# A fused transformer kernel on one NeuronCore: first attention with three packed projections, four moved row sets a block and late division

## The chip, the cores and the metric

The kernel runs on one core of a Trainium2 chip. The metric is the device time of one execution in microseconds; the kernel before takes 709.20 us (median of three runs, 709.16 to 710.09).

## What is computed

x is 16 sequences of 256 tokens with 128 features, all float32. Four layers follow each other, each added to x: an attention (a), a gated feed-forward, a second causal attention with 16 heads, and the same feed-forward again. Only the first attention and the preparation of the feed-forward's weights are touched. The reference of the first, cut:

```
x = x + attn_a(layernorm(x), Wq, bq, Wk, bk, Wv, bv, Wo, bo, freq)
q, k, v = (x @ W + b) split in 2 heads of 64
q, k: features 0..31 of a head stay (content), features 32..63 are rotated (spatial)
      [x1, x2] -> [x1*cos - x2*sin, x1*sin + x2*cos], x1 and x2 of 16 features
score = q k^T / sqrt(64);  attn = softmax(score);  out = (attn v) @ Wo + bo
```

The feed-forward's weights are split into a high and a low part (`whi`, `wlo`) while the first attention runs, and it is counted whether any low part differs from zero.

## The kernel before

x lies in SBUF. The work goes in 8 blocks of two sequences (512 tokens, `TOK`); a block b has two sets of scores, s = 0 and 1, one a sequence. Each engine has its own program, written out by hand (`pe_body`, `act_body`, `dve_body`, `pool_body`), and meets the others at semaphores. A body of block b finishes b, prepares b+1 and begins b+2: `run_inner` runs the bodies of blocks 1 to 6 (1 to 4 in a loop), `..._program` holds what comes before, with the body of block 0, and the last block's part. The queues are in order, so the order of the calls in a body is the order of the work.

In a body of TensorE (`pe_body`, matmuls L220, transposes L449 and L212): scores (b, 1), the k projection of b+1, the transposes of the probabilities (b, 0), k's swapped projection, values (b, 0), v of b+1, the output projection of b-1, scores (b+1, 0), the transposes of xn of b+2, the probabilities (b, 1), two q projections of b+2, values (b, 1). q and k each have two projections: one plain and one with the weight columns of the rotation's halves swapped (`WQR`, `WKR`). VectorE multiplies the first by a cosine row (`straight`, L637) and the second by a sine row (`turned`, L642), GpSimd adds the two (L766). The content features have cosine 1 and sine 0, so they go through all of it.

The softmax: VectorE takes the maxima (L652) and negates and scales them (L657), ScalarE the exponentials with their sums (L553), VectorE the reciprocals (L661), then VectorE normalises head 0 (L666) and ScalarE head 1 (L568), TensorE transposes and ScalarE copies (`act_probT`, L561). There is one set of score banks, so the next scores wait for the exponentials. x of the block gets the output in one add (`dve_update`, L673), and `bo` on GpSimd (L774). Layer norm of b+2: statistics on VectorE (L171, L174), rstd on GpSimd (L207), the shift on VectorE (L189), application on ScalarE (L198, 4 instructions). The weights come in 8 pieces of 704 columns through two stage buffers: ScalarE rounds (L846), GpSimd subtracts (L851), VectorE counts (L857) and writes into the stage buffer while it does, after which SP loads the next piece.

## Time and profile before

| | before |
|---|---|
| median of 3 runs | 709.20 us |
| profiled execution, its time | 709.26 us |
| its span, first to last instruction | 707.5 us |
| mean granted TensorE clock | 0.986 |
| busy, share of the span: TensorE, VectorE, ScalarE, GpSimd | 92%, 70%, 64%, 60% |
| first attention | from the start to about 130 us |

The span is the time of the profiled execution less what lies around it. Busy times of TensorE are modelled at their ends: the distance between two starts says more than a drawn length.

### The profile page before, as it was taken

Reading aid. Unit: us, or ns where it says so; the run is one execution under the profiler, and the core shown is the slowest. Engines: PE = TensorE matmul, PEld = TensorE weight load, DVE = VectorE, ACT = ScalarE, POOL = GpSimd, SP = SyncE. Lnnn points to the kernel's source line nnn. Section 1 sums busy time; section 2 is a strip of 40 time slices with the busy share of each in tenths; the row PEclk is TensorE's granted clock in tenths of the full one; section 3 lists DMA queues with packets and bytes.
Section 4 is the critical chain, followed back from the end, with each engine's and each line's share of the span. In section 5 each row is a group of like instructions: output and inputs, shape, how many; then the busy total and the mean of one; then the engine's idle time right before and its main releaser. Section 6 shows DMA issues by size and latency. Waiting matters only on the chain.

```text
span 707.5 us, 14026 instructions
## 1 busy us (share of the span) xinstructions
PE 652.9 (92%) x4713; PEld 455.8 (64%) x4716; DVE 498.2 (70%) x958; ACT 450.7 (64%) x801; POOL 425.5 (60%) x443
## 2 busy tenths in 40 slices
PE   3789998799999999997999999998989999999997
PEld 1455555477777877675555555555546777787785
DVE  6879998676556778466778888877678565776521
ACT  3678886546665566545676677776765565666664
POOL 4545543368778777533346645654666877778673
PEclk9999999899999999998999999999999999999999
DMA  6101230000000000560467666664221000000001
GB/s 197 41 22 42 54 42 1 1 0 2 1 0 0 0 1 1 188 229 3 138 198 241 198 224 216 224 220 151 84 87 35 0 16 15 15 0 16 16 15 31
DMA packets 33028, 52.47 MB, mean 74 GB/s; under 512 B 4560, under 2 KB 9680, under 8 KB 32976
## 3 DMA queue, kind: packets, MB, share of 16 engines
q1 hardware_dynamic: 32784, 51.53, 23.3%
q8 instruction: 30, 0.49, 0.3%
q10 hardware_dynamic: 192, 0.26, 0.1%
q14 instruction: 22, 0.18, 0.1%
HBM read 27.15 MB, written 24.38 MB: 73 GB/s over the span
## 4 chain that ended last, share of the span: by engine, by line
PE 64%; DVE 16%; ACT 8%; issue 7%; DMA 2%; POOL 2%; DVEq 1%; ACTq 0%; POOLq 0%
PE banks L220 61%; ACT b_prob L1525 4%; DVE xn L182 3%; DVE a_mx L652 2%; ACT a_prob L553 2%; PE banks L212 1%; DVE f_gate L1088 1%; DVE f_h_hi L1091 1%; DVE a_prob L666 1%; DVE f_hidden L1094 1%; PE banks L977 1%; DVE a_straight L637 1%; DVE w_stage L857 1%; ACT f_g_hi L1044 1%; DVE stats L171 1%
## 5 line engine op out<-in xcount | busy, mean ns | idle before, releaser
L1158 POOL TENSOR_TENSOR f_g_lo<-f_gelu,f_g_hi 128x512 fp32r<-128x512 f32 x127 | 162.9, 1292 | 54.1 <-ACT f_g_hi L1044 53.6
L1043 ACT ACTIVATE f_gelu<-banks,cols 128x512 f32<-128x512 f32 x128 | 88.3, 690 | 132.5 <-PE banks L220 110.6
L1624 DVE TENSOR_REDUCE b_segment_max<-banks 128x6 f32<-128x768 f32 x128 | 120.0, 950 | 27.6 <-PE banks L220 27.0
L1741 POOL TENSOR_SCALAR_AFFINE_SELECT b_prob<-b_prob 128x512 f32<-128x512 f32 x128 | 81.7, 639 | 89.2 <-ACT b_prob L1525 88.5
L220 PE MATMUL banks<-f_g_hi,whi 128*128 128x512 f32 x320 | 130.2, 407 | 1.9 <-POOL f_g_lo L1158 1.4
L220 PE MATMUL banks<-f_g_lo,whi 128*128 128x512 f32 x320 | 126.7, 396 | 0.0
L1525 ACT ACTIVATE b_prob<-banks 128x768 f32<-128x768 f32 x128 | 102.4, 807 | 37.5 <-PE banks L220 37.2
L1151 POOL TENSOR_TENSOR f_h_lo<-f_hidden,f_h_hi 128x512 fp32r<-128x512 f32 x60 | 77.6, 1294 | 61.2 <-DVE f_hidden L1094 58.5
L220 PE MATMUL banks<-f_h_hi,whi 128*128 128x512 f32 x256 | 105.2, 411 | 6.2 <-POOL f_h_lo L1151 3.4
L220 PE MATMUL banks<-f_h_lo,whi 128*128 128x512 f32 x256 | 102.0, 398 | 0.0
L1044 ACT ACTIVATE f_g_hi<-banks,cols 128x512 fp32r<-128x512 f32 x128 | 87.4, 683 | 0.0
L1088 DVE SCALAR_TENSOR_TENSOR f_gate<-f_tanh,banks 128x512 f32<-128x512 f32 x64 | 43.3, 677 | 51.5 <-ACT f_tanh L1035 51.5
L220 PE MATMUL banks<-f_xn_split,whi 128*128 128x512 f32 x256 | 71.8, 403 | 1.7 <-DVE f_hidden L1094 1.3
L220 PEld LDWEIGHTS banks<-f_g_hi,whi 128*128 128x128 f32 x320 | 60.3, 188 | 17.2 <-POOL f_g_lo L1158 3.1
L182 DVE TENSOR_SCALAR xn<-X,mv,rstd 128x128 f32<-128x128 f32 (+1 forms) x104 | 70.5, 743 | 0.6 <-POOL rstd L207 0.4
L220 PEld LDWEIGHTS banks<-f_g_lo,whi 128*128 128x128 f32 x320 | 60.3, 189 | 13.2 <-issue 0.2
L220 PEld LDWEIGHTS banks<-f_h_hi,f_h_lo 32*128 32x128 f32 x512 | 37.3, 185 | 43.3 <-ACT b_prob L1525 35.4
L220 PE MATMUL banks<-f_h_hi,f_h_lo 32*128 32x256 f32 (+1 forms) x512 | 55.5, 301 | 8.9 <-ACT b_prob L1525 6.1
L220 PEld LDWEIGHTS banks<-f_h_hi,whi 128*128 128x128 f32 x256 | 48.7, 190 | 23.2 <-POOL f_h_lo L1151 4.5
L220 PEld LDWEIGHTS banks<-f_xn_split,whi 128*128 128x128 f32 x256 | 48.2, 191 | 15.2 <-DVE f_hidden L1094 2.0
L220 PE MATMUL banks<-b_prob,b_values 128*16 128x256 f32 (+1 forms) x1024 | 55.8, 331 | 0.6 <-POOL b_prob L1741 0.6
L220 PEld LDWEIGHTS banks<-f_h_lo,whi 128*128 128x128 f32 x256 | 48.6, 190 | 11.2 <-issue 0.5
(125 smaller groups left out, 1096.4 us busy)
## 6 DMA issues: line engine op xcount, KB each, us to landing
f_h_hi<-b_q_dram SPq DMA_DIRECT2D x16, 512.0 KB, 4.1
f_h_lo<-b_k_dram SPq DMA_DIRECT2D x16, 512.0 KB, 5.2
b_o_dram<-b_o SPq DMA_DIRECT2D x8, 1024.0 KB, 4.4
b_q_dram<-b_q_hi SPq DMA_DIRECT2D x16, 256.0 KB, 3.3
b_k_dram<-b_k_hi SPq DMA_DIRECT2D x16, 256.0 KB, 3.0
w_stage<-in_wF SPq DMA_DIRECT2D x8, 352.0 KB, 3.2
b_q_dram<-b_q_lo SPq DMA_DIRECT2D x8, 256.0 KB, 3.4
b_k_dram<-b_k_lo SPq DMA_DIRECT2D x8, 256.0 KB, 3.1
```

Source lines behind the costliest of these rows:

```text
L182: nc.vector.tensor_scalar(xn[:, s, :], X[:, bass.ds(TILES * t + s, 1), :], mv[:, s, 0:1], rstd[:, s:s + 1], ALU.subtract, ALU.mult).then_i ...
L220: return nc.tensor.matmul(out, lhsT, rhs, start=start, stop=stop)
L553: last = nc.scalar.activation(prob[s][:, h, qt, :], score[:, h, qt * T:(qt + 1) * T], ACT.Exp, bias=nm[s][:, h, qt:qt + 1], scale=SCALE_A, ...
L652: nc.vector.reduce_max(mx[s][:, :, :], score[:, :, :].rearrange("p h (q k) -> p h q k", q=2), AX.X).then_inc(s_mx, 1)
L1043: nc.scalar.activation(gf[c % 2][:, :], z_bank[c % 2], ACT.Gelu, scale=scale).then_inc(s_gf, 1)
L1044: nc.scalar.activation(hi[:, c, :], z_bank[c % 2], ACT.Gelu, scale=scale).then_inc(s_ghi[c % 2], 1)
L1088: nc.vector.scalar_tensor_tensor(out=uu[slot][:, :], in0=th[slot][:, :], scalar=1.0, in1=a[:, :], op0=ALU.add, op1=ALU.mult).then_inc(s_u, 1)
L1151: nc.gpsimd.tensor_tensor(hlo[n.odd][:, c, :], hf[c % 2][:, :], hhi[n.odd][:, c, :].bitcast(F32), ALU.subtract).then_inc(s_hlo[c % 2], 1)
L1158: nc.gpsimd.tensor_tensor(lo[:, c, :], gf[c % 2][:, :], hi[:, c, :].bitcast(F32), ALU.subtract).then_inc(s_glo[c % 2], 1)
L1525: nc.scalar.activation(prob[n % 2][:, p, :, :, :], second_banks(b, p)[:, :, 0:3 * P].rearrange("p b (c q) -> p c b q", c=3), ACT.Exp, scal ...
L1624: nc.vector.reduce_max(seg[:, g, s, 2 * p:2 * p + 2, :], first_pass[:, 2 * p:2 * p + 2, 0:3 * P].rearrange("p b (c k) -> p b c k", c=3), A ...
L1741: nc.gpsimd.affine_select(out=pr, in_=pr, compare_op=ALU.is_ge, fill=0.0, base=0, pattern=[[0, 4], [1, P]], channel_multiplier=-1).then_in ...
```

## The change

Layout: the weights and biases of q and k are packed by kind of feature. One 128-column projection gives the content features of q and k of both heads, one the spatial ones, one the spatial ones with their halves swapped. The first is biased and scaled by ScalarE into `content`; the other two go through VectorE and GpSimd into `spatial`. The factor 1/8 of the scores is multiplied into q's rows by these steps. SP then moves the rows of q and k to the even and odd partitions of `qT` and `kT` in four SBUF-to-SBUF transfers a block (`sp_moves`, 64 partitions by 512 floats, 128 KB each), on whose landing the block's first scores wait.

Softmax: the probabilities are never normalised. The maximum comes out negated. The output projection is done head by head (contraction over 64 rows) into two banks, and x is updated with each, times the head's reciprocal sum as a scalar (8 instructions of 128 columns). The two updates hold the banks that the next content and spatial projections write (`s_half`, `s_done`).

Beside that: the norm's shift is made on GpSimd, from a negated mean; the weight count writes to an unused buffer, so a stage buffer is free once GpSimd has read it; pieces 0 and 1 are rounded ahead of block 0, but subtracted on GpSimd in the middle of block 0 and counted on VectorE at its end. Transfers of the pieces stand in SP's queue behind the moves of a block, and the constant rows of the second attention behind all moves.

```diff
             def sp_program(sp):
...
+                blocks = [Block(i // 2, i % 2) for i in range(BLOCKS)]
+                for n in blocks:
+                    sp_moves(sp, n)
+                    if n.t >= 1:
+                        for piece in blocks[2:4] if n.t == 1 else blocks[n.t + 2:n.t + 3]:
+                            ffn["sp_piece"](sp, piece, False)
...
+            def sp_moves(sp, n):
+
+                t = n.t
+                wait(sp, s_sc, SEQS * (t - 1))
+                sp.wait_ge(s_co, t + 1)
+                for i, to in enumerate((qT, kT)):
+                    sp.dma_start(to[n.odd][0:P:2, :], content[HALF_P * i:HALF_P * (i + 1), :]).then_inc(s_mc, 16)
+                sp.wait_ge(s_ro, t + 1)
+                for i, to in enumerate((qT, kT)):
+                    sp.dma_start(to[n.odd][1:P:2, :], spatial[HALF_P * i:HALF_P * (i + 1), :]).then_inc(s_ms, 16)
...
             def pe_scores(pe, b, s):
                 if s == 0:
-                    pe.wait_ge(s_ro, 2 * (b.t + 1))
+                    pe.wait_ge(s_mc, 16 * MOVES * (b.t + 1))
+                    pe.wait_ge(s_ms, 16 * MOVES * (b.t + 1))
...
             def pe_probT(pe, b, s, h):
-                pe.wait_ge(s_no[h], SEQS * b.t + s + 1)
+                pe.wait_ge(s_ex, UNITS * b.t + HA * s + h + 1)
...
                 pe.wait_ge(s_oc, b.t + 1)
-                token_major(bank, oT, wA[:, WO, :]).then_inc(s_y, 1)
...
+                for s in range(TILES):
+                    for h, bank in enumerate((bank0, bank1)):
+                        at = slice(DA * h, DA * (h + 1))
+                        last = mm(bank[:, s * P:(s + 1) * P], oT[at, s * P:(s + 1) * P], wA[at, WO, :])
+                last.then_inc(s_y, 1)
...
                 if two:
-                    pe_proj(pe, n2, "qr")
-                    pe_proj(pe, n2, "q")
+                    pe_swapped(pe, n2)
+                    if before:
+                        pe.wait_ge(s_half, b.t)
+                    pe_content(pe, n2)
+                    if before:
+                        pe.wait_ge(s_done, b.t)
+                    pe_spatial(pe, n2)
...
                 if two and not is_block(b, 0):
                     ffn["beside"]["act"](act, n2)
-                act_normalise(act, b, 0)
-                if before:
-                    act_out(act, b.after(-1))
-                for h in (1, 0):
+                for h in range(HA):
                     act_probT(act, b, 0, h)
...
+            def dve_update(dve, b, h, bank):
+
                 dve.wait_ge(s_y, b.t + 1)
-                dve.wait_ge(s_bo, b.t + 1)
-                nc.vector.tensor_tensor(xblk(b.t), tiles_of(bank), xblk(b.t), ALU.add).then_inc(s_done, 1)
+                dve.wait_ge(s_in_, b.t + 1)
+                dve.wait_ge(s_half if h else s_bo, b.t + 1)
+                for s in range(TILES):
+                    x = X[:, bass.ds(TILES * b.t + s, 1), :]
+                    last = nc.vector.scalar_tensor_tensor(
+                        out=x, in0=tiles_of(bank)[:, s:s + 1, :], scalar=inv[b.odd][:, s // 2, h, s % 2:s % 2 + 1],
+                        in1=x, op0=ALU.mult, op1=ALU.add)
+                last.then_inc(s_done if h else s_half, 1)
...
                 if is_block(b, 0):
-                    ffn["beside"]["dve"](dve, n2)
+                    ffn["beside"]["dve"](dve, b)
+                    ffn["beside"]["dve"](dve, n1)
...
+                if is_block(b, 0):
+                    ffn["beside"]["pool"](pool, b)
+                    ffn["beside"]["pool"](pool, b.after(1))
+                elif two:
                     ffn["beside"]["pool"](pool, b.after(2))
                 if two:
-                    pool_rope(pool, b.after(2), 0)
+                    pool_rope(pool, b.after(2))
```

How the instructions now stand, at the two places that matter most. TensorE, one whole body inside the bodies of blocks 1 to 6, from the scores (b, 1) on (`a_kT,a_qT` are scores, `xnT,wA` projections of q and k, `wA,xnT` that of v, `wA,a_oT` the output projection). Before:

```order
L220 MATMUL banks<-a_kT,a_qT 128x256 x4
L220 MATMUL banks<-xnT,wA 128x512
L449 MATMUL banks<-ident,a_prob 128x128 x8
L220 MATMUL banks<-xnT,wA 128x512
L220 MATMUL banks<-a_probT,a_v 64x256 x4
L220 MATMUL banks<-wA,xnT 128x128 x4
L220 MATMUL banks<-wA,a_oT 128x128 x4
L220 MATMUL banks<-a_kT,a_qT 128x256 x4
L212 MATMUL banks<-ident,xn 128x128 x4
L449 MATMUL banks<-ident,a_prob 128x128 x8
L220 MATMUL banks<-xnT,wA 128x512 x2
L220 MATMUL banks<-a_probT,a_v 64x256 x4
```

And with the change:

```order
L223 MATMUL banks<-a_kT,a_qT 128x256 x4
L472 MATMUL banks<-ident,a_prob 128x128 x8
L223 MATMUL banks<-wA,xnT 128x128 x4
L223 MATMUL banks<-a_probT,a_v 64x256 x4
L223 MATMUL banks<-wA,a_oT 128x128 x8
L223 MATMUL banks<-a_kT,a_qT 128x256 x4
L215 MATMUL banks<-ident,xn 128x128 x4
L472 MATMUL banks<-ident,a_prob 128x128 x8
L223 MATMUL banks<-xnT,wA 128x512 x3
L223 MATMUL banks<-a_probT,a_v 64x256 x4
```

The two projections that stood around the first transposes are gone, one is added to the pair at the end, and the output projection has eight matmuls in place of four.

VectorE, the body of block 5 (behind the loop). Before, its first half:

```order
L661 RECIPROCAL a_inv<-a_total 128x4
L171 BN_STATS stats<-X 128x6 x4
L174 BN_AGGR mv<-stats 128x2 x4
L666 TENSOR_SCALAR a_prob<-a_prob,a_inv 128x256 x2
L652 TENSOR_REDUCE a_mx<-banks 128x4
L189 SCALAR_TENSOR_TENSOR shift<-mv,rstd 128x4
L657 TENSOR_SCALAR a_nm<-a_mx 128x4
L637 SCALAR_TENSOR_TENSOR a_straight<-banks,cols,cosines 128x512
```

With the change, the whole body:

```order
L174 BN_STATS stats<-X 128x6 x4
L177 BN_AGGR mv<-stats 128x2 x4
L687 TENSOR_REDUCE a_nm<-banks 128x4
L681 TENSOR_TENSOR a_v<-banks,rows 128x512
L692 RECIPROCAL a_inv<-a_total 128x8
L872 TENSOR_SCALAR f_h_hi,f_lo_in_piece<-wlo 128x704
L701 SCALAR_TENSOR_TENSOR X<-banks,a_inv,X 128x128 x4
L687 TENSOR_REDUCE a_nm<-banks 128x4
L701 SCALAR_TENSOR_TENSOR X<-banks,a_inv,X 128x128 x4
L667 SCALAR_TENSOR_TENSOR a_turned<-banks,cols,sines 128x512
L675 SCALAR_TENSOR_TENSOR a_straight<-banks,cols,cosines 128x512
```

The maximum now follows the statistics directly, and the two updates of x enclose the second maximum.

## Rows read from the trace of the kernel before

**Rows 1.** Windows view, bodies 0, 1, 2 to 5 and 6: busy (instructions) by engine.
```profile
core 0: us, PE busy (x) PEld busy (x) DVE busy (x) ACT busy (x) POOL busy (x), PEclk, DMA share, GB/s
24.87:38.00 13.13, 11.68 (x68) 6.70 (x68) 10.41 (x28) 9.94 (x30) 4.56 (x6) 1.00 0.17 55
38.00:54.73 16.73, 13.87 (x79) 8.58 (x77) 12.73 (x29) 11.57 (x33) 8.21 (x7) 0.90 0.10 24
54.73:107.29 52.56, 50.17 (x304) 30.61 (x305) 48.85 (x109) 43.60 (x124) 26.64 (x24) 1.00 0.27 46
107.29:121.06 13.77, 10.98 (x75) 7.17 (x75) 11.56 (x31) 8.93 (x26) 6.25 (x6) 1.00 0.00 0
```
**Rows 2.** Timeline, TensorE, regular body: start us, length us, instruction, idle before.
```profile
83.00 1.04 PE L449 MATMUL banks<-ident,a_prob 128*128 128x128 f32 x8
83.88 1.02 PE L220 MATMUL banks<-xnT,wA 128*128 128x512 f32 x2
...
90.11 1.09 PE L449 MATMUL banks<-ident,a_prob 128*128 128x128 f32 x8 [0.25 <-DVE a_prob L666]
91.03 1.88 PE L220 MATMUL banks<-xnT,wA 128*128 128x512 f32 x4
92.85 1.08 PE L220 MATMUL banks<-a_probT,a_v 128*64 128x256 f32 x8
```
**Rows 3.** Timeline, TensorE, behind the gap of body 1, where nothing holds it.
```profile
46.19 1.08 PE L220 MATMUL banks<-a_probT,a_v 128*64 128x256 f32 x8
...
48.20 1.06 PE L220 MATMUL banks<-wA,a_oT 128*128 128x128 f32 x8
49.19 1.13 PE L220 MATMUL banks<-a_kT,a_qT 64*128 64x256 f32 x8
50.25 0.66 PE L212 MATMUL banks<-ident,xn 128*128 128x128 f32 x4
50.74 1.08 PE L449 MATMUL banks<-ident,a_prob 128*128 128x128 f32 x8
```
**Rows 4.** Timeline, VectorE, regular body.
```profile
82.37 0.58 DVE L666 TENSOR_SCALAR a_prob<-a_prob,a_inv 128x256 f32<-128x256 f32 x2
...
84.00 1.19 DVE L189 SCALAR_TENSOR_TENSOR shift<-mv,rstd 128x4 f32<-128x4 f32 x1
...
88.02 2.03 DVE L666 TENSOR_SCALAR a_prob<-a_prob,a_inv 128x256 f32<-128x256 f32 x2
...
93.45 0.74 DVE L637 SCALAR_TENSOR_TENSOR a_straight<-banks,cols,cosines 128x512 f32<-128x512 f32 x1
```
**Rows 5.** Timeline, GpSimd, regular body: the add of q's two products.
```profile
94.27 1.27 POOL L766 TENSOR_TENSOR a_qT<-a_straight,a_turned 128x512 f32<-128x512 f32 x1 [4.63 <-DVE a_straight L637]
```
**Rows 6.** Timelines, VectorE and TensorE, handover to the feed-forward.
```profile
124.83 0.66 DVE L673 TENSOR_TENSOR X<-banks,X 128x512 f32<-128x512 f32 x1
...
126.61 1.11 DVE L182 TENSOR_SCALAR xn<-X,mv,rstd 128x128 f32<-128x128 f32 x4
...
125.54 2.14 PE L220 MATMUL banks<-f_xn_split,whi 128*128 128x512 f32 x8 [0.33 <-DVE X L673]
```
**Rows 7.** Timeline, ScalarE, regular body: copies, first exponential, applications.
```profile
83.64 1.08 ACT L561 ACTIVATE a_probT<-banks 128x512 f32<-128x512 f32 x2 [0.76 <-PE banks L449]
85.39 0.47 ACT L553 ACTIVATE a_prob<-banks,a_nm 128x256 f32<-128x256 f32 x1 [0.66 <-DVE a_nm L657]
...
87.20 1.65 ACT L198 ACTIVATE xn<-X,shift,rstd 128x128 f32 x4
```
**Rows 8.** DMA issues of the page: count, KB each, median us to landing.
```profile
f_h_lo<-b_k_dram SPq DMA_DIRECT2D x16, 512.0 KB, 5.2
...
b_k_dram<-b_k_hi SPq DMA_DIRECT2D x16, 256.0 KB, 3.0
...
cols<-in_cols SPq DMA_DIRECT2D x1, 13.5 KB, 1.8
```
**Rows 9.** Timelines, VectorE and TensorE, the gap in body 1.
```profile
40.85 0.89 DVE L857 TENSOR_SCALAR_CACHE_REDUCE w_stage<-wlo 128x704 f32<-128x704 f32 x1 [3.01 <-POOL wlo L851]
...
42.92 1.97 PE L449 MATMUL banks<-ident,a_prob 128*128 128x128 f32 x8 [2.73 <-ACT a_prob L568]
```

More of the change, by code:

```diff
@@ L579, in act_body @@
                 nxt = link["next"]
+                if before:
+                    act_out(act, b.after(-1))
                 if two and not is_block(b, 0):
                     ffn["beside"]["act"](act, n2)
-                act_normalise(act, b, 0)
-                if before:
-                    act_out(act, b.after(-1))
-                for h in (1, 0):
+                for h in range(HA):
                     act_probT(act, b, 0, h)
@@ L598, in act_body @@
                     act_exp(act, n1, 0)
+                if two:
+                    act_content(act, n2)
                 if is_block(b, 0):
@@ L663, in dve_normalise @@
[L663 to L673 removed]
+                wait(dve, s_ex, UNITS * (b.t - 1) + HA * (s + 1))
@@ L677, in dve_body @@
                 nxt = link["next"]
-                if not two:
-                    ffn["dve_total"](dve)
-                dve_inverse(dve, b, 0)
                 if two:
@@ L696, in dve_body @@
                     nxt["norm"].dve_apply(dve, FIRST_BLOCK, True)
-                if one:
-                    dve_v(dve, n1)
-                dve_normalise(dve, b, 1)
                 if before:
-                    dve_update(dve, b.after(-1))
+                    dve_inverse(dve, b.after(-1))
+                if two and not is_block(b, 0):
+                    ffn["beside"]["dve"](dve, n1)
+                if before:
+                    dve_update(dve, b.after(-1), 0, content_bank)
                 if one:
                     dve_max(dve, n1, 0)
-                    dve_negate(dve, n1, 0)
-                if two and not is_block(b, 0):
-                    ffn["beside"]["dve"](dve, n2)
+                if before:
+                    dve_update(dve, b.after(-1), 1, spatial_bank)
                 if two:
-                    dve_rope(dve, n2, "qr")
-                    dve_rope(dve, n2, "q")
+                    dve_swapped(dve, n2)
+                    dve_spatial(dve, n2)
                 else:
@@ L774, in pool_body @@
                 nc.gpsimd.tensor_tensor(xblk(b.t), xblk(b.t), row4("bo"), ALU.add).then_inc(s_bo, 1)
-                if one:
-                    pool_rope(pool, b.after(1), 1)
-                if two and not is_block(b, 0):
+                if is_block(b, 0):
+                    ffn["beside"]["pool"](pool, b)
+                    ffn["beside"]["pool"](pool, b.after(1))
+                elif two:
                     ffn["beside"]["pool"](pool, b.after(2))
                 if two:
-                    pool_rope(pool, b.after(2), 0)
+                    pool_rope(pool, b.after(2))
                 if is_block(b, 0):
```

308 lines of the change are left out of this document (144 added, 164 removed).

## The prediction, made before the changed kernel was run

> **What bounds the kernel now.** I cut the first attention into bodies, from one block's second scores to the next block's, at the starts of the score matmuls, and read the windows view of them [rows 1]. Body 0 takes 13.13 us, body 1 takes 16.73 us, the four bodies 2 to 5 take 52.56 us (13.14 us each), body 6 takes 13.77 us. Nothing behind 130 us is touched by the change except one update of x, so the answer lies in these seven bodies, the lead-in and the handover to the feed-forward.
>
> Then the timeline of a regular body. TensorE starts one group after the other with little idle time shown [rows 2], and VectorE is busy 48.85 of 52.56 us [rows 1]. Both are close to full, so I ask what each does when nothing holds it. The distance from start to start gives a group's price. Unheld, the groups cost: a projection 0.91 us (1.82 for two), the transposes of two probabilities 0.88 and 0.92 [rows 2], a value product with the v projection 2.01 (about 1.00 each), the output projection 0.99, scores 1.06, the transposes of xn 0.49 [rows 3]. A body now holds two scores (2.12), four projections (3.64), the probabilities' transposes (1.80), two value products (2.00), v (1.01), the output (0.99) and xn's transposes (0.49): 12.05 us. So 1.09 of 13.14 us are waits, and VectorE causes them: it normalises two tiles in 2.03 us where the same work takes 0.58 in the other half of the body, and its tiny shift takes 1.19 us [rows 4].
>
> **The change, part by part.** *Projections.* Three wide ones instead of four: TensorE loses 0.91 us a body, VectorE two of its four rotation steps (0.74 us each [rows 4]), GpSimd one add of 1.27 us [rows 5].
>
> *Normalisation.* Gone are VectorE's 2.03 + 0.58 us, its negations and shift (1.19 us), and ScalarE's two pairs. In their place x is updated by eight 128-wide steps from PSUM where one 512-wide step took 0.66 us. Four 128-wide steps of another kind took 1.11 us [rows 6], so I take 2.2 us for the eight; the bounds are 1.3 us (eight quarters of 0.66) and 5.3 us (eight of 0.66). VectorE's body becomes 48.85/4 = 12.2, less 2.61 for the normalisation, 1.19 for the shift and 1.48 for the rotations, plus 2.2 - 0.7 for the update: about 8.4 us. It stops being the bound at any value under the upper bound.
>
> *Output projection by heads.* Eight matmuls with 64 rows of contraction instead of four with 128; in the trace each fp32 matmul is two weight loads and two passes, so 16 of each instead of 8. No row shows this shape. The scores are the nearest: 64-row matmuls of the two heads, 8 passes of 256 columns in 1.06 us [rows 3], less than 8 such passes would take one behind the other (a 512-column projection has two passes in 0.91 us, so a 256-column pass takes 0.23 us and eight take 1.8 us). So the two heads run side by side, and the output should take what it took, 0.99 us. Bounds: 0.9 us and 2.1 us (16 at the scores' 0.13 us per pass). The Trainium skill, TensorE: Matmul & The Clock Gate, section LDWEIGHTS, speaks against this part: a load takes as long as it has columns, however few its rows (128 columns: an estimate of 0.107 us by its formula), so 16 loads one after the other would take 1.7 us, and the sum would be 3 us smaller. The scores' rows decide for me.
>
> *The body as it will be.* TensorE's own work is 12.05 - 0.91 = 11.14 us. The other closed path is that of xn: its transposes 0.49, probabilities' transposes 0.92, three projections 2.73, value product 1.00, scores 1.06, then 0.64 until ScalarE copies the next probabilities (83.00 to 83.64), two copies 1.08, exponentials 1.81 (85.39 to 87.20), four applications 1.65 [rows 7], hand-over 0.05 (an estimate): 11.43 us. ScalarE's copies stand ahead of the exponentials in its queue, and xn behind them, which is why this path is longer than TensorE's own. **I take 11.43 us a body.** With an update at its upper bound VectorE would need 11.5 us, about the same.
>
> *Four transfers a block.* The rows of q and k go from SBUF to SBUF, and the next scores wait for them; SP's queue holds nothing but these and one weight piece behind them. From the spatial projection to the scores that need it TensorE has 0.91 + 1.00 + 1.06 + 0.88 + 1.01 + 1.00 + 0.99 = 6.85 us of other work, 7.14 us with the 0.29 us by which the body exceeds its own work. Of that go about 1.1 us until VectorE has the product (a projection is drawn 1.02 us long [rows 2]), 0.82 to GpSimd's start (93.45 to 94.27), 1.27 for its add [rows 4, 5], and an estimate of 0.45 us for the first of the two issues. A landing of up to 3.5 us is therefore hidden. This kind of transfer of 128 KB is not in the trace. Bounds: 1.8 us (13.5 KB) and 5.2 us (512 KB); 256 KB take 3.0 us [rows 8]. I take 2.3 us, hidden with about 1 us to spare.
>
> *Weight pieces in block 0.* Before, GpSimd's late piece holds VectorE for 3.01 us, that holds ScalarE's normalisation, and TensorE stands 2.73 us; the granted clock is 0.90 over this body, and the transposes behind the gap are drawn 1.97 us long, not 1.04 to 1.09 [rows 1, 2, 9]. Now VectorE checks the two old pieces at the end of block 0, which puts 2 x 0.89 us [rows 9] ahead of the next statistics and maximum. An estimate of 0.5 us of it is slack (the statistics end that much before the exponentials' queue is free), so what is late next are the exponentials of body 1, by 1.3 us.
>
> *Sum, with bodies as in [rows 1].* Body 0: 13.13 to 11.43, -1.7. Body 1: 16.73 to 12.75, -4.0. Bodies 2 to 5: 4 x (13.14 - 11.43) = -6.8. Body 6: the transposes for the feed-forward now wait until both halves of an earlier x update are done, and VectorE comes to the second only behind a piece check, statistics, two maxima and the feed-forward's four applications, some 9.5 us after the start. TensorE has 3 us of nothing there, ScalarE's last exponentials come late, and the body ends at 13.8 us as before; 0. The clock fell after the 2.73 us gap in body 1 before, so I add 0.5 us here. Lead-in: the first scores now wait for transfers, +0.2. Handover: the gate products start at 125.54, released by the x update [rows 6]. That update is 2.2 instead of 0.66 us, with little else changed ahead of it: +1.3. The last update, in the feed-forward, has idle VectorE time behind it; 0. Together -1.7 - 4.0 - 6.8 + 0.5 + 0.2 + 1.3 = **-10.5 us**. The profiled execution took 709.26 us (span 707.5), 0.06 us from the median 709.20, so the forecast is 709.3 - 10.5 = 698.8 us.
>
> **Rivals.** *(a) The split output projection pays for each load*: up to its bound of 2.1 us in place of 0.99. TensorE's own 11.14 becomes 12.25 us, 0.8 above the 11.43 path, in six bodies: 4.9 us lost, 703.7. Against it stands the scores' price. It is the mechanism that the Trainium skill's section on LDWEIGHTS would give. *(b) The moves are too slow by a little*: landing at 4 to 4.5 us costs 0.5 to 1.0 us in seven places: 702.3 to 705.8. *(c) Slower than before: the moves set the pace.* From a landing of 3.5 us on, each further microsecond lengthens all seven waits for q and k; at 5.0 us the 10.5 us are used up, and at the 5.2 us of the 512 KB row, with 0.1 us more for the second transfer, the time is 698.8 + 7 x 1.8 = 711.4. For it: two transfers are queued together, beside a 352 KB piece. Against: the size is a quarter of that row's. *(d) The change does not do what it says in block 0*: the gap only moves, since three pieces on GpSimd and two on VectorE still stand before the statistics. Then body 1 stays at about 16 us and the total is 702. *(e) More than forecast*: the xn path is overlapped better, the clock stays up at the handover, and a body is TensorE's bare 11.14 us: 6 x 0.29 + 0.5 + 1.3 = 3.5, so 695.3.
>
> **How the numbers follow.** Forecast 0.52; (a) 0.12; (b) 0.11; (c) 0.05; (d) 0.10; (e) 0.10. A measurement of this kernel can tell a change of about 0.2%, 1.4 us, from none. Faster by more takes the forecast, (a), (d), (e) and nearly all of (b), 0.92; (b)'s slow end gives 0.03 for no difference; (c) gives 0.05. For 8 in 10 I go from 694.5 (e with a little more) to 704.5, which takes in (a), (d) and most of (b).
>
> **What would show it.** In the changed profile: score matmuls (second of a block) 11.3 to 11.7 us apart in bodies 2 to 5; the group of 16 output passes (rows name it wA, a_oT) near 1.0 us from start to start; the moves landing in 2 to 3 us and no wait of TensorE on them; VectorE near 8.6 us a body; no idle of 2.7 us in body 1 and a granted clock of 1.00 there; the handover's update released later than now. I am wrong if TensorE waits for the moved rows in each body, if the output group takes 1.7 us or more, or if bodies 2 to 5 stay above 12.5 us.

## The result, and the profile after

The changed kernel takes 705.79 us (median of 16 runs, 703.44 to 709.21), the kernel before 709.18 us in the same series (16 runs, 707.23 to 710.37). The ratio is 0.9953, with an interval of 0.9941 to 0.9966: faster, by 3.4 us, where 10.5 us were forecast. The time lies above the range.

The profiled execution took 704.96 us (span 703.1, mean granted clock 0.982, before 0.986). TensorE is busy 92% of it as before, VectorE 68% (70%), ScalarE 63% (64%), GpSimd 59% (60%).

First the windows view of the changed kernel, cut at the same instructions as [rows 1]: bodies 0, 1, 2 to 5, 6, and below them the handover, from the second scores of block 7 to the first gate products.
```profile
core 0: us, PE busy (x) PEld busy (x) DVE busy (x) ACT busy (x) POOL busy (x), PEclk, DMA share, GB/s
26.87:38.37 11.50, 10.26 (x68) 6.57 (x67) 5.96 (x15) 10.33 (x29) 7.38 (x9) 1.00 0.43 109
38.37:51.21 12.84, 11.47 (x84) 7.48 (x83) 10.29 (x30) 10.07 (x29) 7.29 (x8) 1.00 0.29 71
51.21:96.73 45.52, 44.65 (x331) 29.57 (x329) 34.95 (x97) 39.04 (x112) 22.71 (x29) 1.00 0.29 71
96.73:112.51 15.78, 10.53 (x81) 7.40 (x79) 10.56 (x29) 7.82 (x23) 4.89 (x5) 0.84 0.53 87
112.51:120.72 8.21, 6.73 (x41) 4.89 (x41) 4.78 (x19) 3.02 (x10) 1.22 (x2) 0.68 0.47 51
```
Set beside [rows 1], and with the handover of before (121.06 to 125.54, 4.48 us):

| stretch | before | forecast | after | off by |
|---|---|---|---|---|
| lead-in, to block 0's second scores | 24.87 | 25.1 | 26.87 | +1.8 |
| body 0 | 13.13 | 11.43 | 11.50 | +0.1 |
| body 1 | 16.73 | 12.75 | 12.84 | +0.1 |
| bodies 2 to 5 | 52.56 | 45.7 | 45.52 | -0.2 |
| body 6 | 13.77 | 14.3 (0.5 for the clock) | 15.78 | +1.5 |
| handover | 4.48 | 5.8 | 8.21 | +2.4 |
| gate products start at | 125.54 | 115.0 | 120.72 | +5.7 |

The bodies came out as forecast: the terms of bodies 0, 1 and 2 to 5 are right within 0.2 us. What is missing up to the gate products lies in the three stretches at the ends. Two of them show a granted clock (PEclk) below 1.00 here, and so does the lead-in, below.

The timeline of TensorE in a regular body of the changed kernel (start, length, instruction, idle time before it in brackets):
```profile
54.19 1.08 PE L223 MATMUL banks<-a_probT,a_v 128*64 128x256 f32 x8
55.20 1.16 PE L223 MATMUL banks<-wA,a_oT 64*128 64x128 f32 x16
56.20 1.03 PE L223 MATMUL banks<-a_kT,a_qT 64*128 64x256 f32 x8
57.45 0.66 PE L215 MATMUL banks<-ident,xn 128*128 128x128 f32 x4 [0.21 <-ACT xn L199]
57.94 1.04 PE L472 MATMUL banks<-ident,a_prob 128*128 128x128 f32 x8
58.81 2.82 PE L223 MATMUL banks<-xnT,wA 128*128 128x512 f32 x6
```
Sixteen passes of 64 rows take 1.00 us from start to start (55.20 to 56.20), what eight passes of 128 rows took in [rows 3] (0.99). The only wait in this body is one of 0.21 us. From the page's DMA part of bodies 2 to 5, count, size and median us to landing of the content moves (the two spatial ones: 2.2 and 2.3):
```profile
a_qT<-a_content SPq DMA_DIRECT2D x4, 128.0 KB, 2.2
a_kT<-a_content SPq DMA_DIRECT2D x4, 128.0 KB, 2.4
```
Next the lead-in, TensorE's timeline of the changed kernel:
```profile
18.44 0.66 PE L215 MATMUL banks<-ident,xn 128*128 128x128 f32 x4 [1.41 <-DVE a_v L681]
21.38 1.28 PE L223 MATMUL banks<-a_kT,a_qT 64*128 64x256 f32 x8 [2.29 <-DMA a_kT<-a_spatial]
22.60 4.34 PE L223 MATMUL banks<-xnT,wA 128*128 128x512 f32 x6
26.87 1.14 PE L223 MATMUL banks<-a_kT,a_qT 64*128 64x256 f32 x8
```
and the first and the last of SP's four issues for block 0 that these scores wait for:
```profile
17.05 0.55 SPq L379 DMA_DIRECT2D a_qT<-a_content  x1
...
18.91 0.60 SPq L382 DMA_DIRECT2D a_kT<-a_spatial  x1
```
TensorE stands 2.29 us for the last of them. Then six passes of a projection take 4.34 us where the same six take 2.82 in the regular body: the granted clock went to its lower level at 22.2 us, for 3.4 us.

Last, the end of body 6 and the handover, TensorE:
```profile
106.81 0.66 PE L215 MATMUL banks<-ident,xn 128*128 128x128 f32 x4 [3.64 <-DVE X L701]
107.30 1.65 PE L472 MATMUL banks<-ident,a_prob 128*128 128x128 f32 x8
...
109.73 1.98 PE L223 MATMUL banks<-a_probT,a_v 128*64 128x256 f32 x8 [0.66 <-ACT a_probT L602]
112.51 2.08 PE L223 MATMUL banks<-a_kT,a_qT 64*128 64x256 f32 x8 [0.80 <-issue]
114.52 1.97 PE L472 MATMUL banks<-ident,a_prob 128*128 128x128 f32 x8
116.42 1.81 PE L223 MATMUL banks<-wA,a_oT 64*128 64x128 f32 x16
118.16 1.08 PE L223 MATMUL banks<-a_probT,a_v 128*64 128x256 f32 x8
120.72 2.14 PE L223 MATMUL banks<-f_xn_split,whi 128*128 128x512 f32 x8 [1.48 <-DVE X L701]
```
and a windows view of TensorE there, cut at the granted clock:
```profile
103.00:107.60 4.60, 0.96 (x9) 1.00 0.46 49
107.60:117.80 10.20, 8.74 (x45) 0.50 0.46 50
```
The wait of 3.64 us that the prediction had seen ("TensorE has 3 us of nothing there") is followed by 10.2 us at 1.2 GHz instead of 2.4. Transposes take 1.65 and 1.97 us (1.04 in the regular body), a value product 1.98 (1.08), scores 2.08 (1.03), output 1.81. I had put 0.5 us on this. VectorE's update that the gates wait for is 2.38 us long (118.28, eight steps; 2.2 priced); four such steps take 1.12 us.

### The profile page after: what moved, and what is told of

Its sections match the earlier page's. It is cut to its first block, busy times and chain, and to the rows that moved or that the text cites. A ratio compares the mean times of both kernels' runs of the same rounds, so it can differ in the third digit from the quotient of the medians.

```text
span 703.1 us, 14140 instructions
## 1 busy us (share of the span) xinstructions
PE 647.1 (92%) x4761; PEld 455.7 (65%) x4764; DVE 477.4 (68%) x937; ACT 442.2 (63%) x777; POOL 417.1 (59%) x448
## 4 chain that ended last, share of the span: by engine, by line
PE 65%; DVE 7%; ACT 7%; issue 4%; POOL 1%; DMA 1%; ACTq 0%; DVEq 0%; POOLq 0%
PE banks L223 62%; ACT b_prob L1540 4%; DVE xn L185 2%; DVE f_gate L1103 1%; DVE f_h_hi L1106 1%; PE banks L215 1%; PE banks L992 1%; ACT f_g_hi L1059 1%; DVE f_hidden L1109 1%; DMA f_h_hi<-b_negative_max 1%; DVE X L701 1%; ACT f_tanh L1050 1%; POOL f_g_lo L1173 1%; DVE b_segment_max L1639 1%; PE banks L472 0%
```

## Experiments

Twelve kernels were run, in four series. Each series had its own runs of the kernel before (medians 708.29, 709.65, 708.64 and 708.98 us), so the kernels are compared by their ratios to it. The last column is the ratio's distance from the changed kernel's 0.9953, times 709.2 us; its uncertainty is 1 to 2 us, since each ratio has an interval of 0.0012 to 0.0025 to either side. Differences of fill_lead, order1 and flag_late from the changed kernel, and of bank_const from bank, are within or at the edge of that. The last two columns are of one profiled execution each. "Last body and handover" runs from block 6's second scores to the gate products in the profile.

| kernel | median us | ratio [interval] | block 0's second scores | last body and handover | against the changed kernel |
|---|---|---|---|---|---|
| changed | 705.79 | 0.9953 [0.9941, 0.9966] | 26.87 | 23.99 | |
| fill_both | 702.27 | 0.9917 [0.9904, 0.9929] | 25.87 | 22.52 | -2.6 |
| fill_lead | 705.17 | 0.9936 [0.9922, 0.9949] | 25.44 | 24.91 | -1.2 |
| fill_six | 703.91 | 0.9921 [0.9899, 0.9943] | 26.99 | 23.71 | -2.3 |
| order1 | 706.55 | 0.9973 [0.9958, 0.9988] | 26.77 | 23.94 | +1.4 |
| bank | 702.34 | 0.9921 [0.9902, 0.9939] | 27.73 | 20.58 | -2.3 |
| flag_late | 705.48 | 0.9946 [0.9932, 0.9960] | 26.57 | 22.43 | -0.5 |
| bank_flag | 702.20 | 0.9878 [0.9859, 0.9897] | 28.40 | 18.38 | -5.3 |
| bank_flag_fill | 697.26 | 0.9831 [0.9815, 0.9847] | 25.63 | 17.77 | -8.7 |
| two_queues | 697.91 | 0.9843 [0.9824, 0.9862] | 25.88 | 17.77 | -7.8 |
| bank_const | 700.94 | 0.9900 [0.9876, 0.9925] | 26.16 | 17.74 | -3.8 |
| best_const | 697.80 | 0.9837 [0.9823, 0.9851] | 24.80 | 18.33 | -8.2 |
| before_pieces | 712.82 | 1.0070 [1.0056, 1.0084] | 24.82 | (19.13) | |

The kernel before has 24.87 us and 18.25 us in these two columns. bank_flag's five runs lie in two groups (699.5 to 699.9 and 702.2 to 702.5 us), so its figure is the least certain: the ratio of the medians is 0.9895, 4.1 us below the changed kernel.

### Does the clock take the gain? fill_both, fill_lead, fill_six

```diff
+ def pe_fill(n):
+     for _ in range(n):
+         mm(pT_bank[0], ident[:, :], wA[:, 0:4, :].rearrange("p w e -> p (w e)"))
...
+                pe_fill(2)
                 pe_scores(pe, b0, 0)
...
                 else:
+                    pe_fill(3)
                     pe.wait_ge(s_done, b.t)
                     nxt["pe_T"](pe, FIRST_BLOCK)
```


> Extra TensorE work whose results nobody reads: two 512-column matmuls (identity by projection weights) before the first scores, three before the feed-forward's first transposes in body 6; all waits stay as in the changed kernel. Clock theory (the halved clock, not the waits, costs most of what was lost against the forecast): granted clock 1.00 from 16 to 125 us, scores (0,1) at 26.1 instead of 26.87 us, the gate products 2.2 to 3 us earlier than the changed kernel's 120.72, time about 702.8 us, and the runs lie closer together. Wait theory (the moved rows and the x update hold TensorE, whatever its clock): scores (0,1) stays at 26.9, the gates move by under 0.5 us, time 705.5.

> The changed kernel with the two dummy products ahead of the first scores alone (of the experiment fill_both, which had three more in body 6 and came to 702.27 us). Theory (the two clock falls cost separately: about 1 us of the lead-in, 2.5 us of body 6 and the handover): second scores of block 0 at 25.9 us instead of 26.87, the clock fall at 106 to 108 us stays with its 10 us, time 704.6 to 705.0 us. Rival (all of the gain of fill_both was the lead-in, the rest was chance): time 702.3 us. Other rival (all of it was body 6): 705.8 us.

> The changed kernel with the three dummy products ahead of the feed-forward's first transposes in body 6 alone, waits unchanged. fill_lead alone came to 705.17 us, both together to 702.27, the changed kernel to 705.79. Theory (nearly all of the gain of fill_both is that the clock does not fall for 10 us behind the wait of 3.64 us): no fall between 104 and 110 us, body 6 of 14.3 to 15.2 us instead of 15.78, time 703.0 to 703.6 us. Rival (the clock falls anyway somewhat later, behind the flag's load of 1.6 us, unless the lead-in is filled as well): time 704.5 to 705.5 us.

The program of all three keeps every wait for a semaphore; dummy work fills part of the idle time. In fill_both the clock fell neither in the lead-in nor at 104 to 110 us, and the time dropped by 0.36% (2.6 us, with an uncertainty of 1.3). The clock fell at 111.4 instead, for 3.4 us, behind a new wait ahead of block 7's second scores ([1.63 <-issue]). fill_lead brought the second scores of block 0 forward by 1.43 us (0.45 of it because the whole execution started earlier: first projections at 10.79, not 11.24), as the theory had it; in body 6 the clock then fell earlier, at 103.9, and the last body and handover took 0.9 us longer. fill_six took the wait before the transposes from 3.64 to 0.86 us with the clock up, and the fall came at 111.6, for 6.8 us:
```profile
106.90 0.66 PE L215 MATMUL banks<-ident,xn 128*128 128x128 f32 x4 [0.86 <-DVE X L706]
...
109.31 1.08 PE L223 MATMUL banks<-a_probT,a_v 128*64 128x256 f32 x8 [0.76 <-ACT a_probT L607]
112.05 2.08 PE L223 MATMUL banks<-a_kT,a_qT 64*128 64x256 f32 x8 [1.66 <-issue]
```
Body 6 of fill_six, from the second scores of block 6 to those of block 7:
```profile
96.82:112.05 15.23, 11.79 (x86) 7.71 (x85) 10.56 (x29) 7.50 (x23) 4.89 (x5) 0.99 0.53 89
```
With the clock up it still takes 15.23 us (fill_both: 15.21), 0.55 less than the 15.78 of the changed kernel. The transposes come 10.08 us after its start here, in fill_both and in the changed kernel, so the length of the wait does not hang on the clock, and most of what body 6 lost is not the clock's.

The falls of the clock that fill_both removed thus cost about 2.6 us. Its theory had the gate products (118.19, 2.5 us earlier) and the time right, but not a clock of 1.00 up to 125 us. For fill_six the rival (the fall comes anyway, later) had the mechanism right, the theory was nearer with the time. What is new is the wait put down to "issue".

### The order of the lead-in: order1

```diff
                 pe_T(pe, b1)
-                pe_scores(pe, b0, 0)
                 pe_swapped(pe, b1)
                 pe_spatial(pe, b1)
+                pe_scores(pe, b0, 0)
                 pe_content(pe, b1)
```
(ScalarE's content of block 1 and VectorE's two rotation steps moved ahead likewise.)

> Lead-in reordered: block 1's swapped and spatial projections stand before the first scores, its content is scaled before the first exponentials. Both theories: TensorE has work while the moved rows of block 0 are under way. Clock theory: no fall of the clock at 22 us, scores (0,1) at about 26.0 instead of 26.87, and the next wait for moved rows (1.24 us before scores (1,0)) goes too: 1 to 2 us less than the changed kernel, 704.3. Wait theory: the first scores still start at 21.4 or later, since the transfers end then; only the 1.24 us wait goes, 704.8.

No gain (ratio 0.9973), though both theories had forecast one. Block 1's projections fill the wait for the moves, and that of 1.24 us before scores (1,0) went too, but everything behind the first scores is then bare: the second scores, at 26.77, stood 2.69 us for the exponentials, and the clock fell at 27.2 instead. In the profiles, dummy work in the gap brought the second scores to 25.44 (fill_lead) where real work moved into it did not.

### Body 6's wait for the x update: bank

```diff
-                    pe_out(pe, b.after(-1))
+                    if two: pe_out(pe, b.after(-1))
+                    else:
+                        pe.wait_ge(s_vr, BLOCKS)
+                        pe_out(pe, b.after(-1), content_bank, misc)
...
                 else:
-                    pe.wait_ge(s_done, b.t)
                     nxt["pe_T"](pe, FIRST_BLOCK)
...
-                else:
-                    pe.wait_ge(s_vr, BLOCKS)
-                    ffn["pe_total"](pe)
                 pe_pv(pe, b, 1)
+                if not two:
+                    pe.wait_ge(s_done, b.t)
+                    ffn["pe_total"](pe)
```


> In body 6 the second head's output product goes to the bank of v's product instead of the one into which the feed-forward's first transposes go, so these no longer wait for the x update; the count of low parts moves behind the value product. Wait theory: the transposes start at about 103.4 instead of 106.81 us, the last exponentials of score set (7,0) 3.7 us earlier, the clock does not fall (no idle of 3.6 us), the gate products start at about 113.5 instead of 120.72, time 699 us. Clock theory alone, without a part for the wait: the same transposes' start but at most 3 us gained, 703 us. If a different wait takes its place (the exponentials or the application of the norm), under 1 us is gained.

The 3.64 us are gone, and the last body with the handover takes 20.58 us instead of 23.99. Up to the gate products this profile gains 2.5 us of these 3.4, since in this execution the clock was down for 6.8 us in the lead-in; by the ratio the time fell by 2.3 us. Of the theories neither came out whole: the wait is gone, but another took its place. TensorE of bank:
```profile
106.62 1.08 PE L223 MATMUL banks<-a_probT,a_v 128*64 128x256 f32 x8 [0.88 <-ACT a_probT L605]
107.70 0.19 PE L223 MATMUL banks<-f_ones,f_lo_in_row 128*1 128x1 f32 x2
110.90 1.29 PE L223 MATMUL banks<-a_kT,a_qT 64*128 64x256 f32 x8 [3.01 <-issue]
```
A wait of 3.01 us now stands ahead of block 7's second scores, and the clock fell at 111.8 behind it, for 3.4 us. Between the two groups TensorE's queue loads the flag that says whether any low part of a weight is not zero.

### The flag's load: flag_late, bank_flag, bank_const

flag_late and bank_flag move the load in TensorE's program:
```diff
-                ffn["pe_load_flag"](pe)
                 pe_scores(pe, LAST_BLOCK, 1)
                 for h in range(HA):
                     pe_probT(pe, LAST_BLOCK, 0, h)
+                ffn["pe_load_flag"](pe)
```


> The changed kernel with one step of TensorE's queue moved: the load of the flag (whether any low part of a weight is not zero) stands behind the second scores of block 7 and the transposes after them, no longer ahead. Theory (the load holds TensorE's queue: VectorE's cast of the flag ends at 109.26 us, and the scores come at 112.51, of which 0.80 us is idle time put down to issue): the scores come about 0.8 us earlier, the clock fall of 107.6 stays, and the end comes 0.5 to 1 us earlier, 705 us. Rival (the gap is that of the exponentials of block 7, which free the score bank at 111.2, and the load only moves the wait): the scores move by no more than 0.2 us or the output group behind the load waits instead, and the time stays at 705.8 us.

> The kernel of the experiment bank (body 6 hands the second head's output group to another bank, so that the feed-forward's transposes do not wait for the x update) with the flag's load moved behind the second scores of block 7 and their transposes. In bank TensorE was idle for 3.01 us before these scores (107.9 to 110.9), and its clock fell at 111.8 for 3.4 us. Theory (the idle time is the flag's load, and the clock fall follows from it): scores at about 108.6 us (the exponentials of block 7 end at 108.55), no clock fall near 112, gate products at 114.5 to 115.5 instead of 118.20, time about 699 us. Rival (the load takes its 2.8 us wherever it stands in the queue): the gap turns up before the output group of block 6 instead, gates at 117.5 or later, time 701.5 to 702.5 us.

Both did the step that was claimed. In flag_late the scores follow the value product at once (111.62, no wait), 15.21 us after block 6's second scores instead of 15.78, so 0.57 us earlier and not 0.8; the time, 0.5 us less, cannot be told from none. In bank_flag the distance from block 7's first scores to its second fell from 7.97 to 5.71 us, and the last body with the handover from 20.58 to 18.38. The clock fell all the same at 109.3, for 3.4 us, so my "no clock fall" was wrong, and the handover kept 7.36 us.

How long the load holds the queue shows in its own rows: of the kernel before,
```profile
L1931 PEldq TENSOR_LOAD <-f_lo_anywhere x1: 489/489/489, 119.2 to 119.2; - x1
```
of the changed one,
```profile
L1946 PEldq TENSOR_LOAD <-f_lo_anywhere x1: 2230/2230/2230, 109.9 to 109.9; - x1
```
(ns, start in us). One instruction, one number, and 1.74 us longer. What changed beside it is SP's queue. Of the kernel before and of the changed one:
```profile
80.46 0.34 SPq L285 DMA_DIRECT2D wB<-in_wB  x1
...
84.53 4.63 SPq L289 DMA_DIRECT2D b_k_dram<-b_constant_rows  x1
```
```profile
99.09 0.58 SPq L288 DMA_DIRECT2D wB<-in_wB  x1
...
103.07 4.65 SPq L292 DMA_DIRECT2D b_k_dram<-b_constant_rows  x1
```
The second attention's constants are issued behind all that SP does for the first. Before, that was one weight piece at 79.9 us; now it is the moves of block 7 at 98 us. The transfers then run for some 20 us (the DMA share is 0.50 from 100 to 120 us, and was 0.00 from 110 to 125 before), over the flag's load. bank_const holds them back until block 7's second scores are done:
```diff
                             ffn["sp_piece"](sp, piece, False)
+                sp.wait_ge(s_sc, SEQS * BLOCKS)
```


> The kernel of bank with one wait more at the end of SP's program: the five transfers of the second attention's constants (the last two issues take 2.6 and 4.6 us on SP, and the transfers run on for some 20 us) start only when the second scores of block 7 are done. Before the change they stood at 80.5 to 102 us; in the changed kernel SP reaches them only behind the last moves, at 99 us, so that they lie over the flag's load, which took 0.49 us before and 2.20 to 2.30 us in every kernel with the change. Theory (the load is slow because these transfers are under way): load of 0.5 us, idle time ahead of the second scores of block 7 down from 3.01 to about 1.2 us (scores 1.8 us earlier behind the value product), time 0.5 to 1.8 us below bank's 702.3. Rival (the load is slow for another reason, its place in the program or the state of TensorE's queue): load of 2.2 us again, gap 3 us, time 702.3.

```profile
L1950 PEldq TENSOR_LOAD <-f_lo_anywhere x1: 486/486/486, 106.6 to 106.6; - x1
```
The theory stands for the load: 0.49 us again, and the idle time ahead of the scores is 1.20 us instead of 3.01. The time is 1.5 us below bank's by the ratios, which is inside the uncertainty of 2.2. Windows view of body 6 and the handover in bank_const:
```profile
96.01:107.48 11.47, 9.15 (x80) 6.69 (x79) 10.56 (x29) 7.61 (x23) 4.89 (x5) 1.00 0.20 46
107.48:113.75 6.27, 4.27 (x41) 3.03 (x41) 4.78 (x19) 2.91 (x10) 1.22 (x2) 1.00 0.41 75
```
Here the handover runs with a clock of 1.00 and a short load, and still takes 6.27 us, not the 5.8 of the forecast. VectorE sets it, without a gap between the reciprocal and the update:
```profile
111.05 0.17 DVE L696 RECIPROCAL a_inv<-a_total 128x8 f32<-128x8 f32 x1
111.31 2.38 DVE L705 SCALAR_TENSOR_TENSOR X<-banks,a_inv,X 128x128 f32<-128x128 f32 x8
```
The update starts 3.83 us after the second scores (3.77 in the kernel before, 5.77 in the changed one), and the gates start 2.44 us after it (0.71 in the kernel before, 2.44 in the changed one).

The Trainium skill, DMA: Bandwidth & Descriptors, section Latency and other measured facts, gives a load of this kind a floor of about 0.6 us. The rows show less, 0.49 us with the transfer engines quiet and 2.2 to 2.3 us beside those transfers; how they delay it (a shared ring, or the memory) no run here tells.

### Putting the parts together: bank_flag_fill, two_queues, best_const

bank_flag_fill is bank_flag with the two dummy products of the lead-in.

> bank_flag with two dummy products of 128x512 ahead of the first scores, which compute nothing that is used and fill the wait for the moves of block 0. Theory (part of what the lead-in lost is TensorE's clock, which fell at 22.2 us behind the wait of 2.29 us and at 19.6 us for 6.8 us in the profile of bank): no clock fall before 100 us, second scores of block 0 at 25.9 us instead of 26.9 to 27.7, and all later bodies as much earlier; time 1 to 1.8 us below that of bank_flag, about 697.5 us. Rival (the lead-in waits for the moves and for ScalarE, whatever the clock): within 0.4 us of bank_flag.

```profile
95.46:106.48 11.02, 9.14 (x80) 6.68 (x79) 10.52 (x29) 7.17 (x23) 4.89 (x5) 1.00 0.57 104
106.48:113.23 6.75, 4.33 (x41) 3.03 (x41) 4.82 (x20) 3.35 (x11) 1.22 (x2) 1.00 0.46 51
```
The clock is at its upper level up to 124 us, and the kernel takes 697.26 us: 0.9831 [0.9815, 0.9847] of the kernel before, faster than both. It is 3.3 us below bank_flag by the ratios (with an uncertainty of 1.8), where 1 to 1.8 were expected. In the two profiles the gate products come 3.4 us earlier: 2.8 of it is the lead-in (28.40 to 25.63; bank_flag's clock was down there for 6.8 us) and 0.6 the handover (7.36 to 6.75 us), which kept the full clock too. One wait shows where the flag's load went:
```profile
109.59 1.16 PE L223 MATMUL banks<-wA,a_oT 64*128 64x128 f32 x16 [0.95 <-issue]
...
113.23 2.14 PE L223 MATMUL banks<-f_xn_split,whi 128*128 128x512 f32 x8 [1.46 <-DVE X L709]
```
two_queues lets ScalarE issue block 0's two content moves, with one dummy product instead of two:
```diff
                 act_content(act, FIRST_BLOCK)
+                act.wait_ge(s_co, 1)
+                for i, to in enumerate((qT, kT)):
+                    act.dma_start(to[0][0:P:2, :], content[HALF_P * i:HALF_P * (i + 1), :]).then_inc(s_mc, 16)
```


> bank_flag_fill with the two content moves of block 0 issued by ScalarE's queue instead of SP's, and one dummy product of 0.94 us ahead of the first scores instead of two. In the changed kernel the four issues of block 0 follow one another on SP (17.05, 17.64, 18.28 and 18.91 us), and the last lands 2.36 us after its start, at 21.27. Theory (the queue of issues sets the first scores): the spatial moves start at 17.3 and 17.9, the last lands at about 20.2, first scores at 20.2 to 20.4 us (bank_flag_fill: 21.21), second ones about 0.9 us earlier, no clock fall in the lead-in; time 0.6 to 1.0 us below bank_flag_fill, about 696.5. Rival (ScalarE's later work, delayed by its two issues of 0.6 us each, sets the next step): second scores at 25.4 us or later, time within 0.3 us of bank_flag_fill. Other rival (transfers issued at once share the engines and land later): first scores at 21 us.

The other rival came out. The four issues went out in 1.5 us instead of 2.5, two and two at once, but three of them took longer to land (DMA issues of this stretch, the queue in the second column, the last number us to landing):
```profile
a_qT<-a_spatial SPq DMA_DIRECT2D x1, 128.0 KB, 2.3
a_qT<-a_content ACTq DMA_DIRECT2D x1, 128.0 KB, 3.1
a_kT<-a_content ACTq DMA_DIRECT2D x1, 128.0 KB, 3.3
a_kT<-a_spatial SPq DMA_DIRECT2D x1, 128.0 KB, 3.0
```
From the end of ScalarE's content step to the first scores it is 3.99 us (17.46 to 21.45) instead of 4.36, and that step itself came 0.44 us later in this execution. That the four transfers share the engines is the rival's reason; the rows show the longer landings alone. First scores and second scores (25.88) are where bank_flag_fill has them within 0.3 us, and no gain can be told.

best_const adds the held-back constants to bank_flag_fill.

> bank_flag_fill (697.26 us) with the same wait for the second attention's constants. Theory: load of the flag 0.5 us instead of 2.25, the idle time of 0.95 us ahead of block 6's output group gone, gate products 6.75 - 0.95 = 5.8 us behind the second scores of block 7, time about 696.4 us. Rival (the load stays at 2.2 us): 697.3 us. If the constants, now between 107 and 130 us, get in the way of the feed-forward's first blocks (they share no engine with it but the SP queue and the transfer engines), the time is above 697.3.

The load took 0.49 us and the wait of 0.95 us is gone, but the clock fell at 106.0, for 3.4 us, behind waits of 0.88 and 0.74 us that bank_flag_fill has as well without a fall, and the handover took 7.32 us. By bank_const's 6.27 the 5.8 of this theory was out of reach even at the full clock. The time, 697.80 us, cannot be told from 697.26.

### The piece order alone: before_pieces

The kernel before, with VectorE's check of each weight piece one body later (as in the change), and nothing else.

> The kernel before with one part of the change alone: VectorE counts a weight piece one body later, so body 1 does not begin with a wait for GpSimd's piece. If the gap in body 1 is a matter of this order alone: no idle of 2.7 us, granted clock 1.00 at 42 us, body 1 at 13.1 to 13.5 us instead of 16.73, time 705.9 us, equal to the whole gain of the full change. If the gap only moves (another engine waits for the same piece): over 708 us.

It is slower than the kernel before, by 0.7%, over the 708 us of the second theory; whether by its mechanism is open. The gap of [rows 9] is gone, the clock stays up, and body 1 takes 14.40 us instead of 16.73. But bodies 2 to 5 take 56.53 us instead of 52.56:
```profile
37.95:52.35 14.40, 12.80 (x78) 7.55 (x76) 13.39 (x27) 11.51 (x32) 8.21 (x7) 1.00 0.01 3
52.35:108.88 56.53, 49.66 (x305) 30.43 (x305) 47.30 (x110) 43.08 (x124) 26.58 (x24) 1.00 0.21 42
```
and TensorE shows a wait in each of them that [rows 2] does not have:
```profile
70.40 1.09 PE L449 MATMUL banks<-ident,a_prob 128*128 128x128 f32 x8 [1.81 <-ACT a_prob L568]
```
So the gap's removal is worth 2.3 us in body 1, while the old body with its full VectorE settles 1 us longer. Which wait holds that slower course up I did not test.

## Why the prediction was wrong

**Right.** The price of a body. *The body as it will be*: 11.43 us forecast, 11.38 measured (45.52/4), and TensorE's own work 11.14 forecast, 11.16 busy; the one wait, 0.21 us, is for xn, the path that the forecast named. Bodies 0, 1 and 2 to 5 are right within 0.2 us, from unheld groups of the old trace. *Output projection by heads*: 0.99 forecast, 1.00 measured, so rival (a) falls, and with it the rule of the Trainium skill (TensorE: Matmul & The Clock Gate, LDWEIGHTS) as I had applied it: sixteen loads of 128 columns one after the other would be 1.7 us. The rows fit two halves of 64 rows that load and run side by side. The same page of the Trainium skill has that too, in its section The mechanism, which I had left out: a load overlaps with matmuls in flight when it goes to other rows of the array. *Four transfers a block*: 2.3 us forecast, 2.2 to 2.4 measured; bodies 2 to 5 show no wait for them (body 0 has one of 1.24 us), so (b) and (c) fall. *Normalisation*: eight update steps 2.38 us (2.2), VectorE 8.74 us a body (8.4), so it is no longer the bound. *Weight pieces in block 0*: body 1 at 12.84 us and a clock of 1.00, so (d) falls.

**Wrong, the term "Lead-in: +0.2"** (measured +2.0). No row stood behind the 0.2; I priced block 0's moves as if they were hidden as in a body. In the lead-in only xn's transposes (0.5 us) lie between them and the scores: four issues of 0.55 to 0.60 us one behind the other, then 2.4 us for the last. Counted from the start of the first projections, the second scores came after 14.06 us before (10.81 to 24.87), after 15.63 in the changed kernel (11.24 to 26.87) and after 14.65 in fill_lead (10.79 to 25.44), where the wait for the moves is still there (0.65 us) and the clock does not fall. By these profiles the moves cost 0.6 us and the clock 1.0. The rest, 0.4, is that the projections began at 11.24 instead of 10.81 in this execution; fill_lead, with the same work ahead of them, began at 10.79. The split is rough: the same distance is 14.0 to 14.9 us in the five profiles in which the clock stayed up.

**Wrong, the term "Body 6: 0, and 0.5 for the clock"** (measured +2.0). The wait was seen, and its length about right (3.64 us, "3 us"); the step that failed is "the body ends at 13.8 us as before". The forecast had the second half of the x update some 9.5 us after the start, but never set this against the kernel before, where the transposes start 8.83 us after it (107.29 to 116.12) and the body ends 4.94 us later; 9.5 and 4.94 would have been 14.4, and not 13.8. Measured were 10.08 and 5.70. So 1.25 us are the later transposes, a wait that lies on the path, and 0.76 lie behind them. Of these the clock has at most 0.55: fill_six and fill_both, with the clock up, need 15.23 and 15.21 us. The 0.5 us for the clock was thus about right here, though no row gave it. flag_late, with the clock down but the load moved away, has 15.21 as well, so these 0.55 us need the low clock and the slow load together.

**Wrong, the term "Handover: +1.3"** (measured +3.7). No part of it was for the clock, which in the changed kernel stays down until 117.8: scores 2.08, transposes 1.97 and output 1.81 us, together 2.6 us above the 1.13, 1.09 and 1.00 of a regular body. bank_const has the same order of work there with a clock of 1.00, and takes 6.27 us against 8.21: about 1.9 us are the clock. The other 0.5 us are the update. 2.2 - 0.66 is 1.5 and not 1.3, and the gates now start 2.44 us after the update's start where they started 0.71 after it before, 1.7 us more. Rival (e) took the 1.3 off again for a clock that stays up, though it was the update's price.

**Not seen at all: SP's queue at the end.** The prediction said that SP's queue "holds nothing but these and one weight piece behind them". It didn't ask what stood behind the last of them: the second attention's constants, which moved from 80 to 99 us and onto the flag's load. In the changed kernel this is part of the 0.8 us of idle time ahead of block 7's second scores; once the larger wait of body 6 is gone it is 1.8 us of idle time (bank against bank_const).

Together the three terms are 5.7 us, the whole difference at the gate products. By the comparisons above about 3.5 of it is the clock (1.0, 0.55 and 1.9; the 0.55 beside the load) and about 2.2 are the waits and the update that were priced too low, with the 0.4 of the later start. fill_both bears the first part out: it leaves the waits in the program, is 2.5 us earlier at the gates, and still has a fall of the clock in its handover (7.31 us, 1.0 above bank_const's). The sizes rest on one profile each. Of the 7.0 us between 698.8 and the median of 705.79, 0.4 lie behind the gate products and 0.8 are the distance of the profiled execution (704.96) from the median; I can't name a cause for these.

bank_flag_fill ends at 697.3 us, 1.5 us below the forecast, but that is no proof of the forecast's sum: it takes away the wait in body 6 that the forecast had counted (11.02 us where 14.3 were forecast), and its lead-in (25.63) and handover (6.75) are still above the terms of 25.1 and 5.8.

## What to carry to other kernels

Price the steady state from unheld groups, but walk the first and the last body of a stage on their own, group by group, against the same stretch of the old trace: a transfer that hides in the loop stands bare ahead of it, a wait that starts later than before makes the stretch end later, and work that followed on a queue is pushed along. Where a forecast leaves TensorE idle (here for 2.3 and 3.6 us), add what its next groups cost at the lower clock to the gap; cheap dummy products in the gap tell the two apart. When work is added to a DMA queue, ask what is behind its last entry and what runs where it lands now.

## What the runs showed of the hardware that I had not expected

- A load of one number from SBUF into TensorE's queue takes 0.49 us with the transfer engines quiet, and 2.2 to 2.3 us while the second attention's constants are under way (256 KB each, DMA share 0.46). While it lasts, no matmul behind it starts (bank: 3.01 us of idle time ahead of the scores; bank_const: 1.20).
- The same sequence of TensorE's instructions with the same waits can keep the clock or lose it: bank_flag_fill had it up until 124.0, best_const lost it at 106.0, both behind waits of 0.88 and 0.74 us. In the lead-in the clock fell in all six profiles in which the first scores waited 2.0 to 2.9 us for the moves, and in none of the five with dummy work there (waits of 0.3 to 1.6 us). The runs of the changed kernel spread over 5.8 us; the two fastest had mean granted clocks of 0.985 (703.44 us) and 0.988 (703.51 us), the slowest 0.977 (709.21 us).
- Four SBUF-to-SBUF moves of 128 KB, issued from one queue 0.6 us apart, land in 2.2 to 2.4 us each; issued in pairs from two queues, in 2.3 to 3.3 us.
- Sixteen fp32 passes with 64 rows of contraction, in two halves of the array, take the 1.00 us of eight with 128.
